# Fused cross-attention in a transformer block: row maxima per head group spread over the whole period, rings of two, mean multiplied in place

## The reference

```
xn = layer_norm(x); q, k, v = xn @ qkv_w.T
x = x + merge(softmax(q k^T * scale) v) @ sa_proj_w.T        # self-attention
xn = layer_norm(x)
q = xn @ q_w.T;  k = ctx @ k_w.T;  v = ctx @ v_w.T           # ctx: 154 rows a batch
attn = softmax(q k^T * scale + (1 - mask) * -10000)
x = x + merge(attn v) @ ca_proj_w.T                          # cross-attention
x = x + gelu(layer_norm(x) @ fc1_w.T + b1) @ fc2_w.T + b2    # MLP
```

## Time and profile before

| what | value |
|---|---|
| median of three runs | 3685.34 us |
| the profiled execution's own time | 3683.99 us |
| its span | 3682.2 us |
| mean granted TensorE clock | 0.94 |
| busy: PE, DVE, ACT, POOL | 3365.0, 2215.5, 1545.2, 1701.3 us |
| fused cross-attention, first to last instruction | 2141 to 2759 us |

### The profile page before, as it was taken

The page is one execution under the profiler, slowest core; times in us unless marked ns, Lnnn a source line. Parts: engine busy times, 40 slices in busy tenths (PEclk is TensorE's granted clock), DMA queues, the critical chain, the costliest instruction groups (busy, mean ns, idle before and its releaser), DMA issues. The chain is left out here.

```text
span 3682.2 us, 52183 instructions
## 1 busy us (share of the span) xinstructions
PE 3365.0 (91%) x16432; PEld 2104.9 (57%) x16432; DVE 2215.5 (60%) x3731; ACT 1545.2 (42%) x2794; POOL 1701.3 (46%) x507
## 2 busy tenths in 40 slices
PE   7998999999999999999999668898876689999999
PEld 6885544444444444444444156556535568888887
DVE  4445878887888888888888125666644632222222
ACT  3230666666666666666666512442422321111111
POOL 0001788888888888888878622342322200000000
PEclk9997999999999999999999887898957889999999
DMA  4547347465465746546553453333315741111110
GB/s 171 180 163 183 71 100 161 87 133 116 96 131 107 155 86 140 115 97 131 107 118 74 106 146 95 116 112 108 90 53 206 263 163 46 46 46 46 46 46 23
DMA packets 178499, 412.01 MB, mean 112 GB/s; under 512 B 20289, under 2 KB 43399, under 8 KB 158831
## 3 DMA queue, kind: packets, MB, share of 16 engines
q1 hardware_dynamic: 156271, 273.87, 24.4%
q0 software_dynamic: 18432, 134.23, 18.2%
q10 hardware_dynamic: 3584, 1.05, 0.1%
HBM read 146.08 MB, written 102.56 MB: 68 GB/s over the span
## 5 line engine op out<-in xcount | busy, mean ns | idle before, releaser
L1591 DVE TENSOR_REDUCE self_part_max<-self_first 128x1 f32<-128x512 f32 x2048 | 1277.9, 676 | 299.9 <-PE self_first L1448 296.6
L1549 ACT ACTIVATE self_expo<-self_second 128x512 f32<-128x512 f32 x2048 | 1068.0, 603 | 690.0 <-PE self_second L1464 656.4
L1397 POOL TENSOR_TENSOR self_pair_sum<-self_expo 128x2048 f32<-128x2048 f32 x192 | 882.8, 4598 | 117.4 <-ACT self_expo L1549 93.9
L1448 PE MATMUL self_first<-self_k,self_q 96*128 96x512 f32 x2048 | 884.6, 439 | 40.9 <-DVE self_part_max L1591 24.2
L1464 PE MATMUL self_second<-self_q,self_k 98*128 98x512 f32 x2048 | 813.4, 400 | 13.5 <-ACT self_expo L1549 13.4
L1448 PEld LDWEIGHTS self_first<-self_k,self_q 96*128 96x128 f32 x2048 | 394.6, 193 | 559.1 <-DVE self_part_max L1591 445.2
L1477 PE MATMUL self_weighted<-self_expo,self_v_sb 128*32 128x512 f32 x4096 | 546.3, 605 | 9.1 <-ACT self_unscaled L1561 6.9
L1464 PEld LDWEIGHTS self_second<-self_q,self_k 98*128 98x128 f32 x2048 | 388.5, 190 | 109.6 <-ACT self_expo L1549 47.7
L1943 DVE CAST mlp_h_high<-mlp_h 128x512 fp32r<-128x512 f32 x128 | 54.7, 427 | 505.6 <-PE mlp_out_sum L61 504.6
L1918 ACT ACTIVATE mlp_h<-mlp_hidden_sum,mlp_b_col 128x512 f32<-128x512 f32 x128 | 88.0, 688 | 601.1 <-PE mlp_hidden_sum L61 601.1
L1397 POOL TENSOR_TENSOR self_half_sum<-self_expo 128x2048 f32<-128x2048 f32 x64 | 292.7, 4579 | 82.9 <-ACT self_expo L1549 82.9
(11 more groups left out here) (165 smaller groups left out, 4130.7 us busy)
## 6 DMA issues: line engine op xcount, KB each, us to landing
self_half_sum<-self_pair_sum POOLq DMA_DIRECT2D x128, 1024.0 KB, 7.2
self_k<-k_t SPq DMA_DIRECT2D x96, 256.0 KB, 9.7
self_q<-q_t SPq DMA_DIRECT2D x93, 256.0 KB, 4.5
cross_q<-cross_r_high SPq DMA_DIRECT2D x256, 64.0 KB, 2.0
qkv_x<-in_x SPq DMA_DIRECT2D x8, 1024.0 KB, 5.4
v<-qkv_v_sb SPq DMA_DIRECT2D x32, 256.0 KB, 2.0
q_t<-qkv_r_high SPq DMA_DIRECT2D x32, 256.0 KB, 2.0
q_t<-qkv_r_low SPq DMA_DIRECT2D x32, 256.0 KB, 2.3
```

Of the source, the lines that this page charges most:

```text
L1397: nc.gpsimd.tensor_tensor(to, expo[:, t % p_slots], expo[:, (t + 1) % p_slots], ALU.add).then_inc(pair_done, 1)
L1448: nc.tensor.matmul(first[:, in_ring[n]], q[0:base, c % q_slots, a, s * P:(s + 1) * P], k[0:base, c // stages_per_group % 2, a, k0:k0 + TOK ...
L1549: nc.scalar.activation(expo[:, t % p_slots, a], second[:, n % ring], ACT.Exp, scale=scale).then_inc(exp_done, 1)
L1591: nc.vector.tensor_reduce(part_max[:, a * SUB + s, k:k + 1], first[:, in_ring[n]], AX_X, ALU.max).then_inc(first_read, 1)
```

## The change

- `first_pass` handles half a head: two matmuls of 154 columns in one bank (`f_ring` = 2 banks named `first`), and DVE's `maxima` takes two maxima a partition (308 elements). There are eight such items for each head group.
- The maxima are turned, split and sent for each head group (`turn_max(t, g)`, four times a tile), and the items are spread: those of groups 2 and 3 of tile t lie between the second passes of groups 0 and 1 of tile t, those of group 0 of the next tile between the second passes of group 3, those of group 1 of the next tile between the matmuls of projections 1 and 2.
- PSUM is shared out anew: `first` 2, `second` 2 (was 3), `weighted` 1, `total` 1, `dense` 2 (was 3).
- `take_weighted` copies the weighted sum to `mean` and waits for the store of the mean two groups before (`out_stored`), no more for the previous mean; `divide` multiplies in place. The reciprocals are a function of their own, `invert`, and some stand between maxima.
- `high_attn(t + 2)` on ACT moves from behind group 1 to behind group 2, between the high parts of results 1 and 2.

```diff
-    s_ring = 3
-    d_ring = 3
+    s_ring = 2
+    f_ring = 2
+    d_ring = 2
...
-        score = m.psum("score", [P, s_ring + 1, TOK])
+        first = m.psum("first", [P, f_ring, TOK])
+        second = m.psum("second", [P, s_ring, TOK])
+        weighted = m.psum("weighted", [P, TOK])
...
+                    ge(pe, first_read, at - f_ring + 1)
+                    for s in range(2):
+                        mm = nc.tensor.matmul(first[:, at % f_ring, s * keys:(s + 1) * keys],
...
                 def take_weighted(t, g):
                     n = groups * t + g
                     act.wait_ge(weighted_done, n_k * (n + 1))
-                    ge(act, mean_done, n)
-                    nc.scalar.activation(unscaled[:], weighted, ACT.Copy).then_inc(weighted_read, 1)
+                    ge(act, out_stored[n % 2], 16 * (n // 2))
+                    nc.scalar.activation(mean[:, n % 2], weighted[:], ACT.Copy).then_inc(weighted_read, 1)
...
                 def divide(t, g):
                     n = groups * t + g
-                    dve.wait_ge(total_done, n + 1)
-                    for part in range(pieces):
-                        cols = slice(part * (TOK // pieces), (part + 1) * (TOK // pieces))
-                        nc.vector.reciprocal(total[:, cols], total[:, cols]).then_inc(inverse_done, 1)
                     dve.wait_ge(inverse_done, pieces * (n + 1))
                     dve.wait_ge(weighted_read, n + 1)
-                    ge(dve, out_stored[g % 2], 16 * (n // 2))
-                    nc.vector.tensor_tensor(mean[:, g % 2], total[:], unscaled[:], ALU.mult).then_inc(mean_done, 1)
+                    nc.vector.tensor_tensor(mean[:, n % 2], total[:], mean[:, n % 2], ALU.mult).then_inc(mean_done, 1)
```

PE's new period:

```diff
+                    for n in range(per_group):
+                        second_pass(t, 0, n)
+                        first_pass(t, 2, n)
+                        if n % 2 == 1 and has_next:
+                            turn(t + 1, n // 2)
...
+                    for n in range(per_group):
+                        second_pass(t, 2, n)
+                        if n == 1:
+                            turn_max(t, 3)
+                        if n == 2:
+                            weigh_both(t, 1)
+                            add_up(t, 0)
+                        if n >= 2:
+                            some(work, 2)
                     if has_next:
-                        rest(result(t + 1, groups - 1))
-                    groups_of(t, groups)
+                        rest(result(t + 1, 2))
+                    work = result(t + 1, 3) if has_next else iter(())
+                    for n in range(per_group):
+                        second_pass(t, 3, n)
+                        if has_next:
+                            first_pass(t + 1, 0, n)
+                        if n == 2:
+                            weigh_both(t, 2)
+                            add_up(t, 1)
+                        if n >= 2:
+                            some(work, 2)
                     if has_after:
-                        for s in range(SUB - 1):
-                            rest(project(t + 2, s))
+                        rest(project(t + 2, 0))
                     if has_next:
-                        firsts(t + 1, project(t + 2, SUB - 1) if has_after else None)
+                        turn_max(t + 1, 0)
+                    weigh_both(t, 3)
+                    add_up(t, 2)
+                    works = [project(t + 2, s) if has_after else iter(()) for s in (1, 2)]
+                    for n in range(items):
+                        if has_next:
+                            first_pass(t + 1, 1, n)
+                        some(works[n // 4], 3)
+                    if has_after:
+                        rest(project(t + 2, 3))
+                    if has_next:
+                        turn_max(t + 1, 1)
```

More of the change, by code:

```diff
@@ L620, in cross_phase @@
         max_split = m.sem("max_split")
-        max_loaded = [m.sem(f"max_loaded{h}") for h in range(halves)]
+        max_loaded = [m.sem(f"max_loaded{g}") for g in range(groups)]
         second_done = m.sem("second_done")
@@ L1001, in period @@
-                    if has_next:
-                        high_result(t + 1, groups - 1)
-                    take_weighted(t, groups - 1)
-                    if has_next:
-                        for half in range(halves):
-                            send_max(t + 1, half)
+                    has_next, has_after = t + 1 < tiles, t + 2 < tiles
+                    for n in range(per_group):
+                        exponential(t, 0, n)
+                        if n == 1:
+                            send_max(t, 1)
+                        if n % 2 == 1 and has_next:
+                            high_turned(t + 1, n // 2)
@@ new lines, in period @@
+                    if has_next:
+                        high_result(t + 1, 1)
+                    if has_after:
+                        high_attn(t + 2)
+                    if has_next:
+                        high_result(t + 1, 2)
+                    for n in range(per_group):
+                        exponential(t, 3, n)
+                        if n == 5:
+                            take_weighted(t, 2)
+                    if has_next:
+                        high_result(t + 1, 3)
+                        send_max(t + 1, 0)
@@ L1008, in _ @@
+                    take_weighted(t, 3)
                 high_attn(0)
@@ L1023, in _ @@
                     high_result(0, g)
-                for half in range(halves):
-                    send_max(0, half)
+                send_max(0, 0)
                 for t in range(tiles):
@@ L1130, in period @@
-                    for g in range(1, groups + 1):
-                        if g == 1 and t > 0:
-                            divide(t - 1, groups - 1)
-                        if g > 1:
-                            divide(t, g - 2)
-                        if has_next:
-                            low_result(t + 1, g - 1)
+                        low_turned(t + 1, chunks - 1)
+                    for n in range(items):
+                        maxima(t, 3, n)
+                        if n == 2:
+                            split_max(t, 2)
+                        if t > 0 and 3 <= n < 3 + pieces:
+                            invert(t - 1, 3, n - 3)
@@ L1174, in _ @@
                     norm(1, s)
-                firsts(0, None)
+                for g in range(2):
+                    for n in range(items):
+                        maxima(0, g, n)
+                    split_max(0, g)
                 for t in range(tiles):
                     period(t)
-                divide(tiles - 1, groups - 1)
+                finish(tiles - 1, groups - 1)
 def self_phase(nc, name, q_t, k_t, v, out, batches):
```

286 lines of the change are left out of this document (147 added, 139 removed).

## The result

The change does not make the kernel faster: 3696.05 us, median of 14 runs (3689.7 to 3704.05), against 3687.69 us for the kernel before (14 runs, 3680.02 to 3697.35). The ratio is 1.0021, 95% interval 1.0011 to 1.0031. I had forecast 3669, faster; the direction was wrong, and the time lies in the range only because the range took in rival C (3699).

What follows compares the result with a forecast made beforehand. TensorE (PE) was busiest, 3365 of 3682 us, but waits between engines set each period. From 3684.0 us, -8.0 - 13.0 + 6.4 + 1.0 - 1.0 = -14.6 gave 3669 us, range 3638 to 3700.

Steps and rivals of the forecast that it cites:

- rival C: Periods 1 to 6: longer slow-clock stretches after idle times cost 5 us each, +30, giving 3699 us; chance 0.20.
- First maxima: Before the first second pass: eight heads of first passes instead of 16, saving 8.0 us.
- Period 0: First period of the cross-attention: no old store to wait for, x ready; 56.5 us against 69.45, -13.0.
- Periods 1 to 5: Steady periods: 66.9 us each plus 4 for one stray slow stretch; 338.5 us against 332.1, +6.4.
- The layout: Step-by-step timing of a steady period at full clock, with the copy waiting 4.3 us for a store; 62.35 us.
- the clock in group 3: Steady period, after the idle time: some 5 us at half speed, costing 2.0 us net.
- short idle times: PE at a group boundary: idle times like the 1.03 us one do not lower the clock.
- Period 6: Next-to-last period, without projection 0 to 3: 62.2 us against 61.2, +1.0.
- Period 7: Last period, all at 1.2 GHz: -7.2 for the copy's wait, 6.2 of first passes not covered, net -1.0 us.
- The maximum: DVE's maxima: one of 308 elements takes 0.45 us, bounds 0.40 and 0.79.
- rival D: DVE's maxima: 308 elements cost as much as 616, 4.4 us a period more, 3705 us; chance 0.05.
- Rival B: Steady periods: the copy's new wait for the store is hidden, 6.2 us less each, 3638 us; chance 0.17.

Runs made afterwards that it cites:

- e3: The kernel before the change with the ring of dense banks at two instead of three, nothing else; 3705.24 us.
- e10: The changed kernel with eighteen extra, overwritten matmuls ahead of the twelve of result 2, filling PE's idle time before group 3; 3686.22 us.
- e1: The changed kernel with the old store of the last group's mean issued ahead of the twelve stack_q DMAs; 3655.20 us, ratio 0.9917.
- e9: The kernel before the change with only the mean multiplied in place and each store issued ahead of its group's DMAs; 3653.29 us.
- e2: The changed kernel with the twelve matmuls of result 2 issued twice in a row; 3702.56 us.
- e5: e1 with the prologue's first 16 uses of dense spread over six banks, plus two guarding waits on PE; 3647.06 us.
- e7: e1 with the last weighted sum (group 3) moved behind the projections and the turned maxima of group 1; 3632.61 us.
- e8: e1, e5, e6 and e7 together, plus the store of group 0's mean ahead of stack_q of group 1; 3625.13 us, ratio 0.9837.
- e6: e1 with each transpose one pair of second passes later and DVE's first two maxima of group 2 ahead of the norms; 3642.36 us.

## Why the prediction was wrong, step by step

- **First maxima, -8.0: wrong in sign, +2.7.** The step counted what the eight heads fewer save and left out what the change does to `dense` there. The first first pass came 8.3 us later (e3, the ring alone: 8.5); 4.5 of it is the ring's, 3.8 a slow stretch that not every execution has. From there to period 0 it took 15.8 us, not 13.5: half first passes that take turns with DVE on two banks need 1.28 us a head from one start to the next, where whole ones needed 1.03 (that the taking of turns is the reason is not isolated). This is 10.7 of the 27 us between forecast and result of the stage.
- **Period 0, 56.5: right,** 55.7.
- **Periods 1 to 5, 338.5: measured 350.9.** The layout was right: x ready 5.25 us into the period (5.2 predicted), the fourth transpose at 12.0 (9.4 plus 2.5 for the clock), SP's DMAs 13.1 behind it (13.05), the copy's wait 4.71 (4.3), the third second pass of group 3 at v + 28.2 (28.05; the steps that I listed behind the copy add up to 5.3 and not 5.1). What was mis-sized is the clock in group 3: I took some 5 us at half speed, costing 2.0, "of which 0.5 is lost again". It was 13.7 us (10.2 to 17.1 in these periods), and cost 4.9 us where I gave 2.0. The piece it slows takes 14.7 us at 2.4 GHz, and my layout has 14.55. e10 also gives the period without it: 64.8 to 66.2, where my sum without the clock of group 3 is 62.35 + 2.5 = 64.85. In five periods I had given the clock there 10 us and 4 more for a stray stretch, and it took 24.5: 10.5 of the 12.4 us too few are this one term. What I had cited from the Trainium skill ("TensorE: Matmul & The Clock Gate", section "HAM oscillation — how this bites in real kernels"), that waits between bursts throttle PE again each time, holds in all five periods of after for both waits, and in group 3 of e10 in two of five. A size for it the rows of before did not hold, and I took it from the stretch there, which had another cause and other work behind it. My remark that short idle times don't bring it was wrong too: in period 4 of before a stretch of 6.8 us (from 2525.06) begins 2.5 us after the same wait of 1.03 us.
- **Period 6, 62.2: 64.8;** e1 has 61.3, so the store's wait is there too. **Period 7, 55.6: 57.6.** Its two terms were -7.2 for the copy's wait and +6.2 for the first passes that move there; e9 and e1 measure them at -6.4 (56.56 to 50.18) and +7.4. (The idle time of 2.35 us does not come three times, as I had read: the three such waits are 6.0 us together.)
- **The maximum** takes 455 ns (0.45 predicted): rival D is false. Rival C, the clock, is what happened in kind; its bound of 0.82 for the mean clock was not reached (0.87) and its price of 5 us a period was double the excess (2.5). Rival B did not happen, but e1 makes it happen and shows its price: I gave 6.2 us a period for it, measured 8.0. I had let it hang on chance whether the store is hidden, where one line of SP's order decides it.

The terms after correction: -8.0 becomes +2.7, periods 1 to 5 +18.8 instead of +6.4, period 6 +3.7 instead of +1.0, period 7 +1.0 instead of -1.0. The gain of period 0 (-13.8) is thus more than eaten, by the ring ahead of it and by a store behind twelve DMAs after it.

## What to carry to other kernels

When a buffer is reused earlier (here by multiplying in place), look for the DMA that frees it in its queue, and count what is issued ahead of it: moving one store ahead of twelve issues turned a loss of 0.2% into a gain of 0.8%. Try the parts of a change alone: the mean in place with its stores moved, without the spread, came out level with both together. When a ring is made smaller, go through every stretch that uses it, the prologue too, and not the steady loop alone. And where PE is the bound, price each new idle time of it with the slow stretch behind it, which here was as large as the wait or larger.

## What the hardware showed that I had not expected

- Two idle times of 1.93 and 2.79 us, with 1.0 us of work between them, came with 13.7 us at 1.2 GHz, which began in the second idle time (2469.0) and in which PE was busy 11.6. The 1.03 us before the change was followed by none in period 3 and by 6.8 us in period 4.
- At the turn of a period, in periods 1 to 5, the longer PE idles for x the more often a stretch at 1.2 GHz begins in that time or right behind it: with 4.2 us in all 25 periods of after, e1, e2, e5 and e10, with 2.1 us in four of five (e7), with 1.1 us in one of five (e8). In e6 it is 1.4 and 1.3 us shortly after one another, and five of five.
- The same program stretch falls to 1.2 GHz in some periods and not in others: e10's periods 1 and 2 have 17.1 and 13.7 us of it, periods 3 to 5 have 6.8, 6.8 and 3.4, with the same instructions.
- More work can cost nothing: 30 matmuls in place of 12 in e10, and the periods in which the clock stayed up in group 3 are 4 to 5 us shorter than those of after.
- A reciprocal of 128 x 128 takes 918 ns before and 943 after, with the same shape and PSUM source; what differs is what runs beside it, and no run here isolates that.
